# Eight tiles to a ring slot, and hats without clip and floor, in two gathering spline convolutions of a graph kernel

## What is computed

```python
def spline_basis(pseudo):                       # pseudo: [E, 3], in [0, 1]
    pos = pseudo * 4
    i0 = clip(floor(pos), 0, 3)
    frac = pos - i0
    ...                                         # 8 weights and 8 of 125 kernel indices per edge

def spline_conv(x, row, col, basis, idx, W, b): # W: [125, Fin, Fout]
    z = einsum('ni,kio->nko', x, W)
    msg = sum_s basis[:, s] * z[col, idx[:, s]]
    return segment_sum(msg, row) / max(deg, 1) + b

h = elu(spline_conv(ones,  ..., stn1_w))        # first convolution
h = elu(spline_conv(h,     ..., stn2_w))        # second: 64 features in, 64 out
t = elu(h @ stn3_w + stn3_b) @ stn4_w + stn4_b
new_pseudo = clip(pseudo + t[col] - t[row], 0.0, 1.0)
out = spline_conv(x, row, col, *spline_basis(new_pseudo), conv_w)   # third: 32 in, 32 out
```

## Time and profile before

| | |
|---|---|
| median of 3 runs | 15551.18 us (15526.23 to 15558.94) |
| the profiled execution | 15572.58 us, span 15570.9 us |
| busy PE, DVE, ACT, POOL | 8388.0, 7182.0, 2542.0, 8827.4 us |
| second convolution, first gather to last | 5283.4 to 7835.5 us |
| third convolution, first gather to last | 8207.0 to 11298.9 us |

### The profile page before, as it was taken

How to read it: one execution, slowest core, us unless ns; L and a number is a source line. 1 busy time by engine, 2 the same in 40 slices (tenths; PEclk the granted TensorE clock), 3 DMA queues, 4 the chain that set the end, 5 groups by cost and what they waited for, 6 DMA issues and landing times. The chain is left out here.

```text
span 15570.9 us, 217238 instructions
## 1 busy us (share of the span) xinstructions
PE 8388.0 (54%) x58520; PEld 7268.8 (47%) x58520; DVE 7182.0 (46%) x16568; ACT 2542.0 (16%) x7161; POOL 8827.4 (57%) x7652
## 2 busy tenths in 40 slices
PE   1346666666466589898863555554520000009996
PEld 1335555555366477777743444444420000009994
DVE  5984444444388666665533455454420000035553
ACT  0002222222100133333321222221200000000001
POOL 0015555555344588888817888888837777732220
PEclk9996666666688799999966667676755555557775
DMA  0000000000511244444413233333311111111110
GB/s 19 0 1 2 2 2 2 2 2 2 8 28 28 60 92 92 93 93 93 91 24 47 45 48 48 47 48 48 48 24 27 27 27 27 26 41 33 33 33 8
DMA packets 1795083, 554.18 MB, mean 36 GB/s; under 512 B 1620582, under 2 KB 1736774, under 8 KB 1794403
## 3 DMA queue, kind: packets, MB, share of 16 engines
q1 hardware_dynamic: 1071972, 306.93, 10.7%
q0 software_dynamic: 241536, 196.63, 7.2%
q10 hardware_dynamic: 481536, 50.16, 3.0%
HBM read 398.94 MB, written 153.86 MB: 36 GB/s over the span
## 5 line engine op out<-in xcount | busy, mean ns | idle before, releaser
L1063 PE MATMUL c_acc<-c_spread_sb,c_basis_sb 128*125 128x256 f32 (+1 forms) x12544 | 2608.7, 381 | 1221.3 <-DVE c_basis_sb L979 1007.2
L1063 PEld LDWEIGHTS c_acc<-c_spread_sb,c_basis_sb 128*125 128x125 f32 x12544 | 2328.6, 238 | 1470.1 <-issue 1277.0
L864 POOL DMA_INDIRECT c_ring<-feat_table,c_at x1568 | 2288.6, 1460 | 464.7 <-issue 463.6
L491 POOL DMA_INDIRECT rec<-rk_rec,rk_place x1568 | 1598.0, 1019 | 1463.8 <-ACT rk_rec L466 1023.7
L558 POOL DMA_INDIRECT g_ring<-gat_table,g_record x1568 | 1623.9, 1036 | 751.9 <-issue 544.8
L864 POOL DMA_INDIRECT c_ring<-hid_table,c_at x1568 | 1745.7, 1113 | 464.7 <-issue 462.2
L1102 ACT ACTIVATE c_sums<-c_acc 125x512 f32<-125x512 f32 (+1 forms) x3136 | 1497.9, 491 | 2381.3 <-PE c_acc L1063 1913.6
L436 PE MATMUL rk_look_ps<-rk_table,rk_lo_t 128*128 128x98 f32 x3136 | 1051.4, 434 | 1116.4 <-ACT rk_table L470 695.4
L964 DVE TENSOR_TENSOR c_spread_sb<-c_mark,c_rin 128x512 f32<-128x512 f32 (+1 forms) x3136 | 1619.1, 550 | 0.0
L436 PEld LDWEIGHTS rk_look_ps<-rk_table,rk_lo_t 128*128 128x128 f32 x3136 | 726.6, 288 | 1485.4 <-DVE rk_before L398 1062.7
L1075 PE MATMUL c_mix<-c_sums,c_w 125*64 125x128 f32 (+1 forms) x18816 | 1135.6, 281 | 401.2 <-issue 293.6
(11 more groups left out here) (320 smaller groups left out, 14079.8 us busy)
## 6 DMA issues: line engine op xcount, KB each, us to landing
c_rin<-rows SPq DMA_DIRECT2D x3136, 42.0 KB
c_rin<-rows SPq DMA_DIRECT2D x3136, 20.0 KB
rows<-c_ring POOLq DMA_DIRECT2D x392, 128.0 KB
at_rin<-rows SPq DMA_DIRECT2D x98, 360.0 KB
rows<-c_ring POOLq DMA_DIRECT2D x392, 72.0 KB
rows<-g_ring ACTq DMA_DIRECT2D x196, 144.0 KB
rec<-rk_rec,rk_place POOLq DMA_INDIRECT x1568
c_ring<-hid_table,c_at POOLq DMA_INDIRECT x1568
```

Of the source, the lines that this page charges most:

```text
L491: pool.indirect_dma_start(out=d.rec, out_offset=bass.IndirectOffsetOnAxis(ap=place[:, u, j:j + 1], axis=0), in_=rec[:, u, j, :], in_offset ...
L864: pool.indirect_dma_start(out=ring[:, u, j, :], out_offset=None, in_=table, in_offset=bass.IndirectOffsetOnAxis(ap=at[:, h, u, j:j + 1], a ...
L1063: last = pe.matmul(acc[pp % BANKS][:, (w % 2) * WN * feats:(w % 2 + 1) * WN * feats], basis[:, q, w, :, :].rearrange("p a b -> p (a b)"), ...
```

## The change

Two edits. First, `SLOT` goes from 4 to 8: a store takes eight tiles, a turn is 32 tiles, `take_places` copies 32 columns. GpSimd no longer waits for a slot's store right ahead of filling it; after each store it waits for the store of the slot before it (`slot_done`) and adds one to a semaphore `done`. `need` counts slots of 8 tiles in place of turns of 16, and SyncE waits once, for `done`. The gathers are outside the loop over passes.

Second, in the third convolution the clip and the cut at zero are gone. `up` and `down` are each raised to a row of five constants with `tensor_tensor` and maximum: `low_end` is 1 at knot 0 and 0 elsewhere, `high_end` is 1 at knot 4 and 0 elsewhere; then comes the minimum. This gives the same hats inside 0 to 1, and the value of the end outside.

```diff
-SLOT = 4
+SLOT = 8
 TILES = RING * SLOT
 TURNS = NT // TILES
-TURN_BITS = (TILES * P).bit_length() - 1
+SLOTS = NT // SLOT
+SLOT_BITS = (SLOT * P).bit_length() - 1
...
+            chain(dve.tensor_scalar(c.low_end[:, :], c.ramp[:, 0:5], 0.0, None, ALU.is_equal))
+            chain(dve.tensor_scalar(c.high_end[:, :], c.ramp[:, 0:5], 4.0, None, ALU.is_equal))
...
-            def store_slot(o, t, u):
-                pool.wait_ge(gathered[u], (o * TURNS + t) * (16 * SLOT) + 16 * SLOT)
+            def store_slot(t, u):
+                pool.wait_ge(gathered[u], t * (16 * SLOT) + 16 * SLOT)
                 pool.sem_inc(pool_turn, 1)
                 pool.dma_start(rows_v[:, bass.ds(t * TILES + u * SLOT, SLOT), :], ring[:, u, :, :]).then_inc(stored[u], 16)
 
-            def later_turn(o, t, h):
-                pool.wait_ge(at_made, o * TURNS + t + 1)
-                for u in range(RING):
-
-                    pool.wait_ge(stored[u], (o * TURNS + t) * 16)
-                    pool.sem_inc(pool_turn, 1)
-                    if u == RING - 1 and not (isinstance(t, int) and t == TURNS - 1):
-                        take_places(t + 1, 1 - h)
-                    gather_slot(h, u)
-                    if u:
-                        store_slot(o, t, u - 1)
-                    else:
-                        store_slot(o, t - 1, RING - 1)
...
+            def slot_done(t, u):
+                pool.wait_ge(stored[u], t * 16 + 16)
+                pool.sem_inc(done, 1)
+
+            def turn_of_slots(t, h, first=False, last=False):
+                pool.wait_ge(at_made, t + 1)
                 pool.sem_inc(pool_turn, 1)
                 for u in range(RING):
...
+                    gather_slot(h, u)
+                    if u == 2 and not last:
+                        take_places(t + 1, 1 - h)
+                    if not (first and u == 0):
+                        store_slot(t if u else t - 1, (u - 1) % RING)
+                    if not (first and u < 2):
+                        slot_done(t if u >= 2 else t - 1, (u - 2) % RING)
...
             def load_windows(o, b):
-                turns = sp.value_load(need[0:1, bass.ds(b, 1)], min_val=1, max_val=TURNS)
-                for u in range(RING):
-                    sp.wait_ge(stored[u], (o * TURNS + turns) * 16)
-                    sp.sem_inc(sp_turn, 1)
+                slots = sp.value_load(need[0:1, bass.ds(b, 1)], min_val=1, max_val=SLOTS)
+                sp.wait_ge(done, slots)
+                sp.sem_inc(sp_turn, 1)
...
-                make_spread(2)
+                make_spread(2, 3)
                 after_step(6)
-                dve.tensor_scalar(pos[:, :, :], pos[:, :, :], 0.0, 1.0, ALU.max, ALU.min).then_inc(seq, 1)
-                make_spread(3)
-                after_step(7)
                 flat = bc(pos[:, :, :].rearrange("p g k -> p (g k)").unsqueeze(2), [P, GW2 * 3, 5])
                 for side, scale, knots, op in ((up, 4.0, c.jm, ALU.subtract), (down, -4.0, c.jp, ALU.add)):
...
                 make_spread(4)
-                after_step(9)
+                after_step(8)
+                for side, floor in ((up, c.low_end), (down, c.high_end)):
+                    dve.tensor_tensor(side[:, :, :], side[:, :, :], bc(floor[:, :].unsqueeze(1), [P, GW2 * 3, 5]),
+                                      ALU.max).then_inc(seq, 1)
+                make_spread(5)
+                after_step(10)
                 three = hat[:, :, :, :].rearrange("p g k j -> p (g k) j")
                 dve.tensor_tensor(three, up[:, :, :], down[:, :, :], ALU.min).then_inc(seq, 1)
-                make_spread(5)
-                after_step(10)
-                dve.tensor_scalar(three, three, 0.0, None, ALU.max).then_inc(seq, 1)
                 make_spread(6)
```

More of the change, by code:

```diff
@@ L275, in _ @@
                 if k == 0:
-                    chain(dve.tensor_scalar(need[:, :], block_fill[:, 1:NB + 1], float(P + TILES * P - 1), float(EP),
+                    chain(dve.tensor_scalar(need[:, :], block_fill[:, 1:NB + 1], float(P + SLOT * P - 1), float(EP),
                                             ALU.add, ALU.min))
                     chain(dve.tensor_copy(c.need[:, :], need[:, :]))
-                    chain(dve.tensor_scalar(c.need[:, :], c.need[:, :], TURN_BITS, None, ALU.logical_shift_right))
+                    chain(dve.tensor_scalar(c.need[:, :], c.need[:, :], SLOT_BITS, None, ALU.logical_shift_right))
                 chain(dve.tensor_tensor(block_size[:, :], block_fill[:, 1:NB + 1], block_fill[:, 0:NB], ALU.subtract))
@@ L807, in flow_conv @@
     at_made = sem(f"{name}_at_made")
+    done = sem(f"{name}_done")
     pool_turn = sem(f"{name}_pool_turn")
@@ L887, in _ @@
-            n = pool.value_load(c.passes[0], min_val=1, max_val=EP // P)
-            with pool.Fori(0, n) as o:
-                take_places(0, 0)
-                pool.wait_ge(at_made, o * TURNS + 1)
+            def slot_done(t, u):
[3 more added lines that the diff above has]
+                pool.wait_ge(at_made, t + 1)
                 pool.sem_inc(pool_turn, 1)
                 for u in range(RING):
-                    gather_slot(0, u)
-                    if u == 0:
-                        take_places(1, 1)
-                    else:
-                        store_slot(o, 0, u - 1)
-                with pool.Fori(0, TURNS // 2 - 1) as i:
-                    later_turn(o, i * 2 + 1, 1)
-                    later_turn(o, i * 2 + 2, 0)
-                later_turn(o, TURNS - 1, 1)
-                store_slot(o, TURNS - 1, RING - 1)
-                for u in range(RING):
-                    pool.wait_ge(stored[u], o * (TURNS * 16) + TURNS * 16)
-                    pool.sem_inc(pool_turn, 1)
+                    gather_slot(h, u)
[5 more added lines that the diff above has]
+                        slot_done(t if u >= 2 else t - 1, (u - 2) % RING)
@@ L908, in _ @@
+            take_places(0, 0)
+            turn_of_slots(0, 0, first=True)
+            with pool.Fori(0, TURNS // 2 - 1) as i:
+                turn_of_slots(i * 2 + 1, 1)
+                turn_of_slots(i * 2 + 2, 0)
+            turn_of_slots(TURNS - 2, 1)
+            turn_of_slots(TURNS - 1, 0, last=True)
+            store_slot(TURNS - 1, RING - 1)
+            slot_done(TURNS - 1, RING - 2)
+            slot_done(TURNS - 1, RING - 1)
         @block.sync
@@ L1044, in _ @@
                 offsets.step(dve, o)
-                dve.tensor_scalar(need[:, :], need[:, :], float(TURNS), float(TURNS), ALU.add, ALU.min)\
+                dve.tensor_scalar(need[:, :], need[:, :], float(SLOTS), float(SLOTS), ALU.add, ALU.min)\
                     .then_inc(need_ready, 1)
@@ L1770, in gnn @@
         c.window_ramp, c.first = sb("window_ramp", [P, NQ, G, WN]), sb("first", [P, NB])
-        c.jm, c.jp, c.up_floor, c.down_floor = (sb(n, [P, 5]) for n in ("jm", "jp", "up_floor", "down_floor"))
+        c.jm, c.jp, c.up_floor, c.down_floor, c.low_end, c.high_end = (
+            sb(n, [P, 5]) for n in ("jm", "jp", "up_floor", "down_floor", "low_end", "high_end"))
         phase(constants)
```

## The result

The changed kernel takes 17,230.86 us (median of 4 runs, 17,116.88 to 17,324.0), the kernel before 15,545.08 beside it: ratio 1.108, 95% interval 1.101 to 1.116. The forecast was 14,740 and faster. The profiled execution took 17,116.88 us for 15,572.6 before, 1544 more.

The account below looks back on a forecast made before the run. GpSimd's unbroken chain of gathers, gaps and stores was taken as the bound, SyncE's loads next. Third convolution -700 us and second -110 make -810, from 15,551 to 14,740 us; range 14,600 to 15,080, 8 in 10.

Parts of the forecast that it names:

- SyncE alone needs 8261.7 + 98 x 24.0: Third convolution: SyncE's loads, at 24.0 us for each of 98 blocks, cannot end before 10,614 us.
- Rival 4: Third convolution: SyncE's loads slow to 26.0 us a block once gathers come without holes beside them; 14,902 us; chance 12%.
- Stores: Both convolutions: 196 eight-tile stores of 1.00 us replace 392 of 0.81, -122 us for each convolution.
- Rival 3: Stores in both convolutions cost in proportion to rows: second gains 0, third -648 us; 14,900 us; chance 8%.
- Waits, the counter, VectorE's +0.34 us a body: GpSimd's and SyncE's new waits cost 0; VectorE's 67 us over 196 bodies stay hidden behind the loads.
- Shut-out gathers: Third convolution: without clip and cut the gathers' excess falls from 792 to 150 us, bounds 50 and 246.
- The count at the cut: Third convolution: with a gather over the cut the next was free in 32 of 32; without, shut out in 16 of 17.
- Rival 1: Third convolution: long gathers stay, because chains of two-input instructions make them; -178 us in all, 15,373 us; chance 7%.
- Rival 2: Third convolution: slower, as the two one-input instructions are openings through which gathers slip; +446 us, 15,997 us; chance 4%.
- The sum: Third convolution -700 us, second -110, together -810: median from 15,551 to 14,740 us.
- the second half of rival 1: Third convolution: clip and cut block GpSimd only for their own length, at most 90 us; whole change some 320 us, 15,285.

Follow-up runs that it names:

- a3: The changed kernel once more, on a chip without the 0.7-us waits: 3.9% faster than the kernel before, ratio 0.961.
- e3: The changed kernel with SLOT = 4 (four-tile stores, new hats and counter kept): 0.984 of the kernel before.
- e2: The kernel before with only the change's hats (no clip, no cut, two maxima), on the old ring: 0.985 of the kernel before.
- e7: e3 with the third convolution's scalar_tensor_tensor written as tensor_tensor, on a chip without the waits: 169 gathers over 2.5 us; no time or ratio in the text.
- h1: f2 with clip and cut put back in place of the maxima: 14,146 us, for 14,125 of f2 on the same chip.
- f2: e3 with the third convolution's eight spreads of a body all behind its bases, on a chip without the waits: 0.9536 of the kernel before.
- g1: f2 with SLOT = 8, on a chip with the waits: 81% of SyncE's third-convolution records have the wait; no time or ratio in the text.
- g4: The changed kernel with GpSimd waiting for each store to land before the next gather, on a chip with the waits: SyncE at 35 us a block.

## Why the prediction was wrong

**The step that failed** is the one on SyncE: "SyncE alone needs 8261.7 + 98 x 24.0", and 23.8 a block in the second, whatever GpSimd does. That took the pace of the engines behind GpSimd (SyncE, and TensorE at 23.2) as their own. In the second convolution SyncE needed about 240 us a block while GpSimd gathered (first loads at 5321 and, nine blocks later, at 7483), and 23 after. Rival 4 named the right mechanism in kind, SyncE slower beside unhindered gathers, but for the third convolution, and had 26.0 us a block, read from a single one; the kernel before had no row of an eight-tile store beside unhindered gathers. It did show the 0.7-us waits in 6% of SyncE's records, and I never looked at what lies between its loads. Without the waits the step holds: in a3 SyncE takes 23.9 us a block from first load to last (24.4 counted from the first gather).

**Stores.** Forecast 1.00 us from bounds of 0.81 and 1.62; measured 0.94, so four more rows a partition cost 0.13 us. Worth 133 us a convolution for 122. Right. Rival 3 falls.

**Waits, the counter, VectorE's +0.34 us a body.** Taken as nothing. For the waits and the counter e3 against e2 (0.984 and 0.985) shows no cost. VectorE's busy time in the third convolution rose by 61 us (1617 for 1555), 0.31 a body; both of those runs have it, so that it cost nothing is argued from VectorE's idle half.

**Shut-out gathers.** "The excess of 792 us falls to ... 150" measured 648, because the cause was wrong. Clip and cut don't shut gathers out: without them they stay (e2, e3, e7), with them they are gone once the spreads stand last (h1). The count at the cut was near enough true of the trace and no proof of cause: where a gather stood at the cut also fixed how far into the body the next one began. The changed kernel, with no cut, shows such a count too. Take the start of the plane in the bodies without an earlier long gather: with a gather over it the next was free in 51 of 51, without one it was shut out in 14 of 22. In e3 the same count is no rule at all (free in 49 of 61, shut out in 7 of 22). Rival 1 had the mechanism, if "chains of two-input instructions" is read as chains of these kinds; its argument against (the second convolution has chains too) failed, since not every chain does it. Rival 2 said slower, and slower came, but by another way: without the two instructions e2 and e3 had 121 and 128 long gathers for 158, and 672 and 711 us of excess where it needed over 1024. That it came out slower is no merit of rival 2.

Of the Trainium skill, "SBUF — State Buffer", section "Who interferes with whom", says that `tensor_tensor` contends only with GpSimd's reads, and that in a mode with both ports VectorE blocks GpSimd for one whole instruction. A block of one instruction's length doesn't fit e7's trace: the gather of 6.67 us stood beside a dozen instructions, the longest of about 1.2 us, all `tensor_tensor`. Whether a gather's read or its write is what waits, no run here shows.

**The sum.** Forecast -700 and -110. On a chip without the waits the change is 0.961, and the forecast was 0.948: there the second convolution gained 219 us against four-tile stores (2391 for f2's 2610), more than the 110, while 500 us of the third's gain did not come, as the excess stayed. That the ratio comes near the forecast there is in part luck, since the two misses have opposite signs. With the waits the second lost 1644. A forecast of one number could not hold both. One slip stands in the working: the second half of rival 1 is some 320 us in one place and 15,551 less 15,285, which is 266, in another; the first leaves out VectorE's longer body.

**What stays open:** what the 0.7-us wait is, why it comes on some chips, and why eight tiles in one store make it constant where two stores of four in a row cost 297 us. That the starving takes large stores and unhindered gathers together is shown (g1, g4, and the records inside long gathers); what they crowd out is not. Eight tiles with the spreads last on a chip without the waits was not tried.

## What to carry to other kernels

A consumer's pace read beside a producer holds only for the load that the producer puts on the chip then; before making the producer faster or its transfers larger, look at the steps between the consumer's own instructions, down to register moves, for waits that nothing explains. Compare on more than one chip when a change makes transfers larger: the same kernel was 3.9% faster on one chip here and 10.8% slower on another. And an association counted in one trace, even 32 of 32, is no cause until the suspect has been taken out alone; interleaving independent work into a dependent chain, done to fill an engine's stops, can shut out the engine that lived from those stops.

## What the runs showed of the hardware that was not expected

On three of the six chips of the experiments, and in the first two traces, SyncE and TensorE wait 0.7 us or its multiples ahead of instructions without a semaphore while GpSimd gathers: in the second convolution 6 to 9% of SyncE's records with four-tile stores, 39 to 55% with eight-tile ones, in g1's third 81%; on the other chips 0.4% or less in either convolution. It needs gathers under way: while a gather was shut out (the kernel before and the changed one), or while GpSimd waited for its store to land (g4), 0.1% of the records or none had it. A gather that takes 0.95 us by itself took up to 7.3 us (e7) beside VectorE's instructions, in a stretch of `tensor_tensor` alone; with the independent spreads moved behind the dependent steps none took over 2 us.
